# Local-score turns with 32 mask matmuls each, condition rows and bias products in column groups, and a new order of the steps

## The reference, cut to what matters

```python
ada = t_emb @ w_ada + b_ada                  # 6 rows of 256 per batch
xm = expmap0(xn * (1 + sc_msa) + sh_msa)     # then q, k, v, 16 heads, softmax
ff = plin(plin(xm, w_f1, b_f1), w_f2, b_f2)  # no nonlinearity between the two maps
...
base = (j > i) & (j <= i + W)                # local attention: 64 keys back
sc = where(mask, Q K^T / 4, -inf); p = softmax(sc); local = p V
lmask = arange(N_LATENTS) <= arange(S) // 4  # attention to pooled latents
...
out = sum_e w_e * (relu(z Wi^T + (z A_e) B_e) Wo)
```

## Time and profile before

| What | Value |
|---|---|
| Median of 3 runs | 1249.25 us (1247.89 to 1251.9) |
| The profiled execution's own time | 1248.74 us |
| Its span, first to last instruction | 1246.9 us |
| PE busy | 1158.8 us (93%), 13948 matmul records |
| DVE / ACT / POOL busy | 853.8 (68%) / 706.5 (57%) / 238.3 us (19%) |
| Mean granted PE clock | 0.978 |

### The profile page before, as it was taken

How to read it: one execution, slowest core, us unless ns; L and a number is a source line. 1 busy time by engine, 2 the same in 40 slices (tenths; PEclk the granted TensorE clock), 3 DMA queues, 4 the chain that set the end, 5 groups by cost and what they waited for, 6 DMA issues and landing times.

```text
span 1246.9 us, 34256 instructions
## 1 busy us (share of the span) xinstructions
PE 1158.8 (93%) x13948; PEld 824.2 (66%) x13948; DVE 853.8 (68%) x3321; ACT 706.5 (57%) x1429; POOL 238.3 (19%) x336
## 2 busy tenths in 40 slices
PE   6977769999999999999999999999999999999996
PEld 2544445676667677767777677766777667777764
DVE  6858768886986857767677788767577785552332
ACT  1456676658766654757376755757465754434221
POOL 2302022022112210141113111041112120210111
PEclk9978889999999999999999999999999999999998
DMA  9220001000010100000010101000010000000000
GB/s 317 96 81 13 22 15 28 23 29 13 28 36 19 36 2 28 27 27 28 9 46 2 31 15 32 14 23 11 3 32 6 28 16 19 11 11 19 20 10 9
DMA packets 27231, 38.51 MB, mean 31 GB/s; under 512 B 3489, under 2 KB 21281, under 8 KB 27073
## 3 DMA queue, kind: packets, MB, share of 16 engines
q1 hardware_dynamic: 25280, 34.29, 8.6%
q10 hardware_dynamic: 1792, 2.03, 0.5%
HBM read 31.62 MB, written 4.29 MB: 29 GB/s over the span
## 4 chain that ended last, share of the span: by engine, by line
PE 74%; DVE 10%; ACT 9%; issue 4%; POOL 1%; DMA 1%; ACTq 0%; DVEq 0%; POOLq 0%
PE psg L436 44%; PE psq L436 16%; PE pso L436 7%; PE psg L439 7%; ACT PQ L1379 4%; DVE nm L929 2%; DMA QK<-in_w 1%; ACT QK L1379 1%; POOL M L1719 1%; ACT JA L1390 1%; DVE TU L926 1%; DVE lp L926 1%; ACT M L1379 1%; DVE JD L942 0%; DVE R L926 0%
## 5 line engine op out<-in xcount | busy, mean ns | idle before, releaser
L1379 ACT ACTIVATE PQ<-psq 128x2048 f32<-128x2048 f32 x112 | 210.2, 1877 | 86.0 <-PE psq L436 85.5
L1744 POOL TENSOR_TENSOR R<-R,rhoT 128x256 f32<-128x256 f32 x128 | 90.7, 729 | 429.0 <-ACT R L1379 429.0
L436 PE MATMUL psq<-QK 32*128 32x128 f32 (+5 forms) x3360 | 129.6, 303 | 0.2 <-DMA QK<-in_w 0.2
L436 PE MATMUL psg<-zT,WiT 128*128 128x256 f32 x512 | 123.8, 385 | 2.8 <-DVE R L926 2.7
L436 PE MATMUL pso<-PQ,Vg 128*32 128x256 f32 (+2 forms) x2048 | 111.3, 349 | 12.3 <-ACT PQ L1379 9.5
L436 PE MATMUL psg<-WoT,R 128*128 128x256 f32 x512 | 115.6, 381 | 0.0
L436 PEld LDWEIGHTS psq<-QK 32*128 32x128 f32 (+2 forms) x3360 | 93.0, 165 | 22.7 <-issue 13.7
L929 DVE TENSOR_REDUCE nm<-psq 128x16 f32<-128x2048 f32 (+1 forms) x48 | 92.7, 1931 | 21.8 <-PE psq L436 21.4
L436 PEld LDWEIGHTS psg<-zT,WiT 128*128 128x128 f32 x512 | 93.5, 192 | 18.3 <-DVE R L926 3.9
L436 PEld LDWEIGHTS psg<-WoT,R 128*128 128x128 f32 x512 | 95.2, 190 | 14.9 <-issue 2.6
L1379 ACT ACTIVATE R<-psg 128x512 f32<-128x512 f32 x64 | 38.1, 595 | 117.8 <-PE psg L436 117.6
(11 more groups left out here) (224 smaller groups left out, 2281.6 us busy)
## 6 DMA issues: line engine op xcount, KB each, us to landing
bcB<-ada_rows SPq DMA_DIRECT2D x16, 384.0 KB, 3.4
bcA<-ada_rows SPq DMA_DIRECT2D x15, 384.0 KB, 3.5
X<-in_x SPq DMA_DIRECT2D x16, 256.0 KB, 5.0
XR<-in_x SPq DMA_DIRECT2D x16, 256.0 KB, 2.7
out<-XR SPq DMA_DIRECT2D x16, 256.0 KB, 2.2
QK<-NMT SPq DMA_DIRECT2D x128, 3.0 KB
WiT<-in_WiT SPq DMA_DIRECT2D x1, 1024.0 KB, 4.9
WoT<-in_WoT SPq DMA_DIRECT2D x1, 1024.0 KB, 7.4
```

What stands on the lines that cost most here:

```text
L436: return e.matmul(o, lhsT, rhs, start=start, stop=stop, skip_group_check=True)
L1379: return e.activation(o, i, func, **kw)
L1744: e.tensor_tensor(R4, R4, rhoT[:, :], ALU.mult).then_inc(*pool_moe.mark(b, f"r{f}{j}"))
```

## The change

1. **Turns.** The blocks of turns 0 and 2 are laid out anew, so that the two blocks of 192 query columns stand side by side. One matmul per tile then writes both masks, with the mask slice repeated by a zero stride, and one more the block of 128: 32 mask matmuls of 384 and 128 columns. Turn 1 gets 16 of 2 x 128 and 16 of 256 columns. The columns of a tile are 512 a turn as before. `values` takes the new offsets through `turn_of`; its matmuls stay the same.
2. **Condition rows.** `condT` is padded to 32 columns; the six matmuls put the three 512-column parts into three column groups (32 rows each) of one bank. DVE adds biases with two instructions in place of six; the constant 1 of the scale rows comes from two new columns of `hsel`. The bias rows load with three transfers of 64 KB, not one of 48 KB, and `hsel` loads ahead of `wqkv`.
3. **Bias products.** The eight b_f1 matmuls go to four column groups as four partial sums (new step b1p); ACT copies these to `VB` and squares `b1c` with a sum (b1q); one matmul with a selecting column adds and replicates them (b1w), one more does the norm (b1b).
4. **The order.** The strings of all five engines are new, over the whole program.

The diff, cut to its core (of each order table one line of an engine before and after; `hs` in the inputs gets two columns: 1 for the partitions 64 to 95, and 1 for 0 to 31):

```diff
-        "AA*AAn*qqqq*******hhn*qqqqa*naaaaaaaooohhoaqqaaqaaqaaaoonohohqNqqqFFaaaaaaaaooppopoppphhmaaaaaaaamoomNnm",
...
+        "A*An*qqqq*******hh**a*anaaqqqqaaaaoonohhoaqqaaqaaqaaaoonohohqqNqqFFaaaaaaaaooppopoppphhmaaaaaaaamooNmnmF",
...
-        "PnnnnnPqq**nnnn*hhnP*qnnqannnaaaaaooohhffaffqafaffananqannnooPohNNhffNNfNfqqfaaffggaggaagaoggoppopffppff",
...
+        "PnnnnnqqP***hh**nnannanaqPqaannannnooohhffaffqafaffananqannnooPohNNhffNNfNfqqfaaffggaggaagaoggoppoppffpf",
...
-        "n*****wAxwxxxAAnnN*nnNxnmNnxNnxmewNnxmNnewxmNnemwxNnxmewNnmewxNnmewNnmNewnmNewmewNmewNmNewmewmewmewee",
...
+        "*****nwxwxxxAAAnNn*nnNxnmNnxNnxmewNnxmNnewmxnNemwxNnxmewNnmewxNnmewNnmNewnmewNmewNmNewmNewmewmewmewee",
...
-        hsel = sb("hsel", [128, 6])
+        hsel = sb("hsel", [128, 8])
...
-        condT = sb("condT", [128, 2, 16])
+        condT = sb("condT", [128, 2, 32])
...
-        adaR = TU[0:16, 0, :], TU[0:16, 1, :], JM[0:16].rearrange("p t n -> p (t n)")
-        bada = U[0][:, 0:768], U[1][0:16, 0:768]
+        adaR = TU[0:96, 0, :]
+        bada = U[0][:, 0:768], U[1][0:96, 0:512]
...
-        turns = [[(0, 0, 0), (0, 1, 192), (1, 0, 320)], [(1, 1, 0), (3, 1, 128)], [(2, 0, 0), (2, 1, 192), (3, 0, 320)]]
+
+        turns = [[(0, 0, 0), (1, 0, 192), (0, 1, 384)], [(1, 1, 0), (3, 1, 128)], [(2, 0, 0), (3, 0, 192), (2, 1, 384)]]
...
-        quad = Banks([psq], dve_ada.at(0, "a3"))
-        po, pg = Banks([pso], dve_ada.at(0, "a5")), Banks(psg)
+        quad = Banks([psq], dve_ada.at(0, "a1"))
+        po, pg = Banks([pso]), Banks(psg)
...
-                for j, o in enumerate((psq[0:16, 2, :], psq[0:16, 3, :], pso[0:16, :])):
-                    yield
-                    if j:
-                        for c in range(2):
-                            w.wait_ge(*loads[f"wada{c}1"])
-                    for c in range(2):
-                        last = mm(o, condT[:, c, :], wada[c][:, 512 * j:512 * j + 512], c == 0, c == 1)
-                    last.then_inc(*pe_ada.mark(0, f"r{j}"))
+                yield
+                for c in range(2):
+                    w.wait_ge(*loads[f"wada{c}1"])
+                for c in range(2):
+                    for j in range(3):
+                        last = mm(psq[32 * j:32 * j + 32, 2, :], condT[:, c, :], wada[c][:, 512 * j:512 * j + 512], c == 0, c == 1)
+                last.then_inc(*pe_ada.mark(0, "r"))
...
+                bank = take(pg, ("b1p",), act_late.at(0, "b1p"))
+                w.wait_ge(*loads["b1c"])
+                for h in range(2):
+                    for j in range(4):
+                        f = 4 * h + j
+                        last = mm(bank[32 * j:32 * j + 32, :], b1c[:, f:f + 1].broadcast_to([128, 32]), wx[h][:, j, :], h == 0,
+                                  h == 1)
+                last.then_inc(*pe_late.mark(0, "b1p"))
+                yield
                 bank = take(pg, ("b1w",), act_late.at(0, "b1x"))
-                w.wait_ge(*loads["b1c"])
-                for f in range(8):
-                    last = mm(bank[:, :], b1c[:, f:f + 1].broadcast_to([128, 128]), wx[f // 4][:, f % 4, :], f == 0, f == 7)
-                last.then_inc(*pe_late.mark(0, "b1w"))
+                w.wait_ge(*loads["hsel"])
+                w.wait_ge(*act_late.at(0, "b1p"))
+                mm(bank[:, :], hsel[:, 3:4].broadcast_to([128, 128]), VB[:, :], True, True).then_inc(*pe_late.mark(0, "b1w"))
                 yield
                 bank = take(pg, ("b1b",), act_late.at(0, "b1b"))
-                for f in range(8):
-                    last = mm(bank[:, 0:2], b1c[:, f:f + 1].broadcast_to([128, 128]), b1c[:, f:f + 1].broadcast_to([128, 2]),
-                              f == 0, f == 7)
-                last.then_inc(*pe_late.mark(0, "b1b"))
+                w.wait_ge(*pool_setup.at(0, "ones"))
+                w.wait_ge(*act_late.at(0, "b1q"))
+                mm(bank[:, 0:2], bb1[:, :].broadcast_to([128, 128]), Vg1[:, 0, 0:2, 16], True, True
+                   ).then_inc(*pe_late.mark(0, "b1b"))
...
-                    for c, kt, q0 in turns[v]:
-                        n = 128 if kt else 192
-                        for i, j, r, o in tiles():
-                            m = 96 - 32 * j
-                            mm(psq[o, i, q0:q0 + n], unit(r), MK[r, m:m + n], q0 == 0, False)
-                    if v == 1:
-                        for i, j, r, o in tiles():
+                    n = 128 if v == 1 else 192
+                    for i, j, r, o in tiles():
+                        m = 96 - 32 * j
+                        mm(psq[o, i, 0:2 * n].rearrange("p (h n) -> p h n", h=2), unit(r),
+                           MK[r, m:m + n].unsqueeze(1).broadcast_to([32, 2, n]), True, False)
+                    for i, j, r, o in tiles():
+                        if v == 1:
                             m = 128 - 128 * (j % 2)
                             mm(psq[o, i, 256:512], unit(r), MLT[r, m:m + 256], False, False)
+                        else:
+                            m = 96 - 32 * j
+                            mm(psq[o, i, 384:512], unit(r), MK[r, m:m + 128], False, False)
...
-                w.wait_ge(*loads["bada1"])
-                for j, i in enumerate((psq[0:16, 2, :], psq[0:16, 3, :], pso[0:16, :])):
-                    yield
-                    w.wait_ge(*pe_ada.at(0, f"r{j}"))
-                    for h in range(2):
-                        n, o = 2 * j + h, slice(256 * h, 256 * h + 256)
-                        k = 256 * (n % 3)
-                        stt(adaR[j][:, o], i[:, o], float(n in (1, 4)), bada[n // 3][0:16, k:k + 256], ALU.add,
-                            ALU.add)().then_inc(*s.mark(0, f"a{n}"))
+                for j in range(3):
+                    w.wait_ge(*loads[f"bada1{j}"])
+                w.wait_ge(*loads["hsel"])
+                for h in range(2):
+                    yield
+                    o = slice(256 * h, 256 * h + 256)
+                    w.wait_ge(*pe_ada.at(0, "r"))
+                    stt(adaR[:, o], psq[0:96, 2, o], hsel[0:96, 6 + h:7 + h], bada[1][:, o], ALU.add,
+                        ALU.add)().then_inc(*s.mark(0, f"a{h}"))
...
+                        w.wait_ge(*loads["adaB"])
...
-                load(e, "bada1", bada[1], A["b_ada"][768:1536].partition_broadcast(16))
+                for j in range(3):
+                    load(e, f"bada1{j}", bada[1][32 * j:32 * j + 32, :], A["b_ada"][512 * j:512 * j + 512].partition_broadcast(32))
...
+                w.wait_ge(*pe_late.at(0, "b1p"))
+                copy(VB[:, :], pg.where["b1p",][:, :]).then_inc(*s.mark(0, "b1p"))
+                e.activation(b1c, b1c, ACT.Square, accum_out=bb1[:, :]).then_inc(*s.mark(0, "b1q"))
...
+                load(e, "hsel", hsel[:, :], A["hsel"])
...
-                    w.wait_ge(*dve_ada.at(0, f"a{2 * j + 1}"))
-                    e.dma_start(scratch[:, 512 * j:512 * j + 512], adaR[j]).then_inc(*loads[f"ada{k}"])
+                    w.wait_ge(*dve_ada.at(0, "a1"))
+                    e.dma_start(scratch[:, 512 * j:512 * j + 512], adaR[32 * j:32 * j + 16, :]).then_inc(*loads[f"ada{k}"])
```

More of the change, by code:

```diff
@@ L346, in program @@
         xr_in, out_done = [landing(f"d_xr{i}") for i in range(2)], [landing(f"d_out{i}") for i in range(2)]
[L348 to L350 removed]
+        pe_ada = sig("pe_ada", "bc", "r")
+        dve_ada = sig("dve_ada", "c0", "c1", "c2", "a0", "a1")
+        act_late = sig("act_late", "W0", "W1", "b1p", "b1q", "b1w", "b1x", "b1b")
         pool_setup = sig("pool_setup", "zero", "ones", "ident", "identb")
         pool_late = sig("pool_late", "mask", "wgkv", "gt0", "gt1", "w2sq")
[L353 removed]
+        pe_late = sig("pe_late", "W0", "W1", "b1p", "b1w", "b1b", "w2sq")
         dve_late = sig("dve_late", "gv0", "gv1", "g00", "g01", "g10", "g11", "ys", "yq", "dz", *rs("d"), "dT", "Bh", "Bl", "Bm", "Bst")
```

121 lines of the change are left out of this document (58 added, 63 removed).

## The result

The changed kernel took 1238.22 us, median of 4 runs (1237.09 to 1238.95), beside 1248.76 us (4 runs, 1247.89 to 1251.9) for the kernel before: ratio 0.991, 95% interval 0.9891 to 0.993. That is faster by about 11 us, inside the forecast range of 1221 to 1241 us, and 8 us above the likeliest time of 1230 us. The profiled execution has a span of 1236.6 us at a mean granted PE clock of 0.975; before, 1246.9 us at 0.978.

A forecast was written before the change was run, and what follows sets the result against it. PE's own work was taken as the limit from 210 to 1200 us (97% busy). 1248.7 - 9.9 (masks) - 9.2 (start) = 1229.6 us, with 0.5 us to the median 1230 us; range 1221 to 1241 us.

The forecast's parts named there:

- I take 0.37 us for the new turn: 0.58 - 0.37 = 0.21 us: Local turns' mask phase on PE: 32 matmuls take 0.37 us where 48 took 0.58, saving 9.9 us over 48 turns.
- The straight line: Mask phase interpolated from one pass (0.36 us) to three (0.58): 0.47 us a turn, only 5.3 us saved.
- rival 4: Mask phase goes by columns and stays 0.58 us; only the start counts, 1240 us; chance 0.06.
- I count all 9.9 us: Local turns, nearly all between 210 and 1200 us: the masks' whole PE saving of 9.9 us comes off the time.
- So I count 9.2 us: Start, condition rows and bias products: 14.0 us of PE work become 4.8, all 9.2 us counted, zero as other end.
- near 43 us: Sign at the start: the first scores of batch 0 start near 43 us, not 58.
- rival 1: Start hidden: PE reaches batch 0's heads sooner and waits for DVE; masks alone count, 1239 us; chance 0.15.
- its output's transposes end before 73 us: Sign in batch 0's attention: the output's transposes on PE end before 73 us, not 83.
- the order at zero with 3 us of loss and 7 us of gain: New order at the start: moved batch 1 steps against two more table loads, net zero, bounds +3 and -7 us.
- rival 3: From 57.9 to 210 us, less PE work lengthens the lower clock level by 14 us: 5 us lost, 1235 us; chance 0.10.
- the forecast 19.1 us: Total saving forecast on PE: 9.9 us from the masks and 9.2 us from the start.
- Rivals 2 and 5: Batch 0's attention hides 7.0 us moved steps, 1223 us (0.12); new bare psq waits in all batches, 1262 us (0.05).

The follow-up runs named there:

- e4: Changed kernel with its mask written in three passes again (48 matmuls), all else as changed: 1243.52 us, ratio 0.9925.
- e3: Kernel before, old turns, 48 mask matmuls and old order, with only the condition rows and bias products new: 1250.74 us, ratio 0.9981.
- e11: The changed kernel once more, with no edit, timed beside other kernels on one chip: 1236.44 us, ratio 0.9891 to the kernel before.
- e1: Kernel before with only the new turns and their 32 mask matmuls, old order and old start: 1240.94 us, ratio 0.9907.
- e9: Changed kernel with one pass of 16 mask matmuls a turn that add zeros, local masks left out: 1238.32 us, one run.
- e10: Changed kernel with the same masks cut into four passes, 64 mask matmuls a turn: 1251.41 us, one run.

## Why the prediction was right, and where it was off

**Masks, as forecast on PE.** The step "I take 0.37 us for the new turn: 0.58 - 0.37 = 0.21 us" held: 0.37 us, and 0.200 to 0.215 us off each score step, 9.8 us over 48 turns, of which 1 us goes with the layout. The straight line (0.47) and rival 4 (0.58) are out. What was too simple is "I count all 9.9 us": from k2 to k15 5.6 us of 8.0 came off the time (5.8 in the new order), some 6 to 7 us in all. Masks alone, though, gave a ratio with 11.6 us (0.9907 of 1252.24, interval 9.9 to 13.3). Of the 8.9 us in span, 1.4 are at k0, ahead of the first changed turn, where that execution has 3.3 us less of the lower level; and of the 2.2 us between k0 and k2, 1.5 go with 3.4 us less of it.

**Start, the step that failed.** "So I count 9.2 us" was right about the work (1.85, 1.85 and 0.86 us for the condition step, b1p and b1w, 0.28 us for b1b, the first scores at 42.4 us for "near 43 us") and wrong about what comes off the end. At k0 5.6 us are left in the new order and none in the old one (196.0 for 195.9 us, with 6.8 us more at the lower level, some 3 us as an estimate). In the old order DVE's heads take a part, which is rival 1, and the clock may have taken the rest. In the new order the lead goes in steps, read from the timelines: 15.5 us at the scores, 9.9 at the last values of batch 0, 7.5 at its output's transposes, 5.6 at k0. On the first of these the steps q of batch 1 and the two table loads lie between the exponentials; on the second the output part is 10.6 us long instead of 8.1 (64.00 to 74.56; 73.9 to 82.02), and DVE's heads of batch 1 stand in it. The timeline of DVE in the changed kernel:

```profile
67.00 0.26 DVE L947 RECIPROCAL kf<-psg 128x16 f32<-128x16 f32 x1 [3.14 <-PE psg L440]
67.18 0.73 DVE L935 TENSOR_TENSOR U<-U,hf 128x512 f32<-128x512 f32 x1
67.83 0.41 DVE L935 TENSOR_TENSOR Vg<-U,hf 128x256 f32<-128x256 f32 x1
68.17 0.68 DVE L935 TENSOR_TENSOR U<-U,hf 128x512 f32<-128x512 f32 x1
68.77 0.41 DVE L935 TENSOR_TENSOR Vg<-U,hf 128x256 f32<-128x256 f32 x1
...
73.73 0.69 DVE L935 TENSOR_TENSOR ST<-ST,ky 128x512 f32<-128x512 f32 x1
```

Four heads operations, about 2 us (67.18 to 69.11), stand between the reciprocal and the chain whose last row PE waits for with its 5.89 us. DVE before, where the chain follows its reciprocal at once:

```profile
76.48 0.26 DVE L935 RECIPROCAL kf<-psg 128x16 f32<-128x16 f32 x1
76.77 0.42 DVE L923 TENSOR_TENSOR ST<-psg,kf 128x256 f32<-128x256 f32 x1
```

The other 0.5 us goes with the clock: the transposes at 65.88 us take 1.94 us, at the lower level, and the same eight took 1.06 us before. The forecast "its output's transposes end before 73 us" was missed by 2.4 us. I had counted the order at zero with 3 us of loss and 7 us of gain; with the old masks both together are worth 8.7 us at one clock (e4) and the start alone 1.4 us (e3), and the order alone was not run.

**The clock, rival 3.** It did not come where it was expected: the granted clock from 57.9 to 210 us is 0.87 in both profiles, and up to k15 they have the same time at the lower level. But the clock took something at the end, 13.7 us at the lower level for 6.8, about 3 us; e11 shows that an execution can do without, and the profile would then be near 1233.5 us, as e11's 1233.8. In span, 8.8 us of the forecast 19.1 are missing: 3.6 us of the start (9.2 less 5.6), 2.5 us of the middle (9.9 less 7.4) and 2.7 us at the end. In the middle the new order's 1.4 us, counted at zero, cover a part of what the masks fell short by.

**Rivals 2 and 5.** The moved steps did not run wholly in idle time, and no new bare waits on `psq` came: PE stays at 97% from 210 to 1200 us.

**Left open.** Why the second pass is free and the third and fourth are not. Whether the new beginning brings the longer low stretch at the end, and the masks alone the higher clock of e1's runs. Which waits in the first two batches could be shortened by an order made for both halves of the start was not tried.

## What to carry to other kernels

A matmul taken off an engine that was 97% busy was worth 70 to 80% of its time here, and one taken off an engine in a stretch with waits may be worth much less: follow a lead from milestone to milestone, not only to where the work was. Where parts of a change act on the same stretch, time each alone and both together, and compare them at one mean clock or in a stretch at full clock: here the medians alone made two gains that add look as if they did not. When an idle matrix engine falls to the lower clock ahead of a dense stretch or in the last batch, a few matmuls that nobody reads, put into its waits, can be worth a good part of a tuning step (here some 6 us for both places together, where the whole change brought 11).

## What the runs showed of the hardware

- 16 matmuls of 32 x 32 tiles cost 0.37 us with 512 columns per tile (e9), 32 the same (after), 48 cost 0.55 to 0.58 us (e4, before) and 64 cost 0.69 us (e10), with the columns unchanged. The page "TensorE: Matmul & The Clock Gate" of the Trainium skill (Part 3, Measured speedup vs the span model) gives about 4 ns per further tile. By that, as an estimate from the page's figure and the 0.213 us of 512 columns at full level, and carried over to several passes, which the page does not do, 16, 32, 48 and 64 matmuls would take 0.27, 0.34, 0.40 and 0.47 us; the trace is near it for 32 and above it for 16, 48 and 64.
- The same program at the same point of its span (1209.8 us) has one execution at 13.7 us of the lower clock and another at 6.8 us. Further stretches of about 3.4 us, near 16 us and near 352 us, are in some profiles and not in others, with the old and the new order alike. Each costs about 1.5 us, a little under half its length, so two or three of them could make up the spread between runs (1247.89 to 1251.9 us before).
- Six matmuls into three column groups (two to a group) and eight into four (also two to a group) take 1.85 us each: in these two the depth of a group counts, not the number of groups.
